# Values of an attention step as one product of 512 queries instead of two of 256

## The reference

```python
# block 1, causal
s = einsum('bhqd,bhkd->bhqk', q, k) / sqrt(8); s = where(causal, s, -inf)
o = einsum('bhqk,bhkd->bqhd', softmax(s), v)
x = x + o @ Wo; then layer norm, 512-wide gelu MLP
# block 2, not causal
attn = softmax(einsum('bhqd,bhkd->bhqk', q, k) / sqrt(8))
ao = einsum('bhqk,bhkd->bhqd', attn, v)
# then layer norm and a mixture of 8 experts, 2 chosen for each token
```

## Time and profile before

| | us |
|---|---|
| median of 3 runs | 1733.78 |
| lowest and highest run | 1729.83, 1735.24 |
| profiled execution, from first to last instruction (its own time is shown as this span alone) | 1730.5 |
| TensorE, VectorE, ScalarE busy in it | 1456.8, 1251.8, 1169.9 |
| first attention, values from/to | 116.7 to about 593 |
| second attention, values from/to | about 790 to 1468.4 |

### The profile page before, as it was taken

One profiled execution on the slowest core, in us unless ns is written; L12 is line 12 of the kernel. 1 busy time (PEld: TensorE's weight loads), 2 busy tenths in 40 slices (PEclk: granted clock), 3 DMA queues, 4 the chain that ended last, 5 costly groups with the idle time before them and its releaser, 6 DMA issues.

```text
span 1730.5 us, 39194 instructions
## 1 busy us (share of the span) xinstructions
PE 1456.8 (84%) x15185; PEld 663.6 (38%) x15185; DVE 1251.8 (72%) x1974; ACT 1169.9 (68%) x2373; POOL 339.9 (20%) x386
## 2 busy tenths in 40 slices
PE   5679999999998888748999999899988989899940
PEld 3334444444444455402222222222222223788930
DVE  6787877878776156688999999799979973342444
ACT  7537777867777655506998998789877887433421
POOL 5300000000000156400000001100112331441455
PEclk9869999989989899957999999999999999999985
DMA  4612101111110344320133332011200130767941
GB/s 137 199 57 64 68 33 60 44 57 55 54 51 19 95 125 136 118 89 8 45 116 121 125 113 81 18 47 63 75 17 32 55 125 30 208 212 240 277 139 56
DMA packets 127770, 158.46 MB, mean 92 GB/s; under 512 B 14432, under 2 KB 100448, under 8 KB 127328
## 3 DMA queue, kind: packets, MB, share of 16 engines
q1 hardware_dynamic: 118368, 130.77, 24.0%
q0 software_dynamic: 9216, 25.18, 4.1%
HBM read 90.90 MB, written 68.96 MB: 92 GB/s over the span
## 4 chain that ended last, share of the span: by engine, by line
PE 24%; DVE 17%; issue 9%; DMA 8%; ACT 4%; POOL 2%; SPq 1%; another core or an unknown queue 0%; ACTq 0%; POOLq 0%; DVEq 0%
DVE row_max L632 14%; PE bank L599 6%; DMA sorted_in<-v_all,slots 5%; PE banks L1439 4%; PE banks L1429 4%; PE banks L575 4%; PE banks L543 2%; ACT probs L686 2%; DMA qk_parts<-parts 1%; POOL probs L1250 1%; DMA parts<-sorted_in 1%; PE banks L1420 1%; PE banks L1384 0%; PE banks L330 0%; PE banks L1331 0%
## 5 line engine op out<-in xcount | busy, mean ns | idle before, releaser
L632 DVE TENSOR_REDUCE row_max<-banks 128x2 f32<-128x1024 f32 (+3 forms) x896 | 939.5, 1104 | 140.4 <-PE banks L549 74.1
L686 ACT ACTIVATE probs<-banks 128x512 f32<-128x512 f32 (+3 forms) x1792 | 879.8, 551 | 192.0 <-PE banks L575 90.1
L599 PE MATMUL bank<-probs,v_ones 128*32 128x256 f32 (+3 forms) x7168 | 539.2, 378 | 19.8 <-ACT o_sums L697 16.8
L543 PE MATMUL banks<-k_work,q_work 48*128 48x512 bf16 (+3 forms) x1792 | 368.1, 383 | 76.3 <-DVE row_max L632 57.3
L575 PE MATMUL banks<-q_work,k_work 51*128 51x512 bf16 (+3 forms) x1792 | 387.2, 375 | 43.1 <-DMA q_work<-max_T 25.4
L575 PEld LDWEIGHTS banks<-q_work,k_work 51*128 51x128 bf16 x1792 | 102.5, 93 | 414.4 <-ACT probs L686 322.6
L599 PEld LDWEIGHTS bank<-probs,v_ones 128*32 128x32 f32 x7168 | 147.5, 109 | 257.8 <-ACT probs L686 183.8
L724 POOL DMA_DIRECT2D heads_out<-o_sums x64 | 35.7, 558 | 1015.2 <-ACT o_sums L697 1015.2
L543 PEld LDWEIGHTS banks<-k_work,q_work 48*128 48x128 bf16 x1792 | 95.1, 96 | 142.7 <-DVE row_max L632 105.8
L2007 ACT ACTIVATE rope<-banks,expert 128x256 f32<-128x256 f32 x184 | 72.2, 475 | 114.8 <-PE banks L1429 89.8
L1429 PE MATMUL banks<-rope,expert 128*128 128x256 f32 x368 | 90.6, 391 | 7.8 <-issue 7.2
(11 more groups left out here) (194 smaller groups left out, 1104.9 us busy)
## 6 DMA issues: line engine op xcount, KB each, us to landing
expert<-expert_rows SPq DMA_DIRECT2D x46, 578.0 KB
qk_parts<-parts SPq DMA_DIRECT2D x64, 256.0 KB, 3.4
heads_out<-o_sums POOLq DMA_DIRECT2D x64, 256.0 KB, 4.0
sorted_in<-front SPq DMA_DIRECT2D x21, 512.0 KB, 6.3
q_work<-qk_parts SPq DMA_DIRECT2D x64, 128.0 KB
k_work<-qk_parts SPq DMA_DIRECT2D x64, 128.0 KB
parts<-sorted_in SPq DMA_DIRECT2D x46, 128.0 KB
q_work<-qk_parts SPq DMA_DIRECT2D x64, 64.0 KB
```

Source lines behind the costliest of these rows:

```text
L543: last = pe.matmul(to[:, par, 0:width], q[r:r + M0, pair, qt * P:(qt + 1) * P], k[r:r + M0, pair, kh * G:kh * G + width], start=True, stop ...
L599: last = pe.matmul(bank[7][32 * j:32 * j + 32, c0 + part * w:c0 + (part + 1) * w], v_ones[i % QB][:, kt, j, :], prob_slots[:, (e + j) % RI ...
L632: dve.tensor_reduce(row_max[:, qt, 2 * pair:2 * pair + 2, kh], self.buf_of("chunk", g, c)[:, :, 0:width], AX.X, ALU.max).then_inc(s["chunk ...
L686: act.activation(prob_slots[:, e % RING, 0:width], banks46[:, e % EXP_BANKS, 0:width], ACT.Exp, scale=SCALE).then_inc(s["exps"], 1)
```

## The change

`PARTS`, the number of products into which a step's values are cut, goes from 2 (PAIRS) to 1. Each part covers `(G - c0) // PARTS` queries, so a full step's product has 512 moving columns instead of 256. The one part is issued behind the second unit of the next step; before, one part was issued behind each unit. Semaphore counts follow PARTS everywhere else in the code.

```diff
-PARTS = PAIRS
+PARTS = 1
...
         for pair in range(PAIRS):
             order.append(("unit", 0, PAIRS * k + pair))
             some((PAIRS * k + pair + 1) * len(stream) // (PAIRS * len(steps)))
-            if k:
-                order.append(("values", 0, PAIRS * (k - 1) + pair))
+            if k and pair % (PAIRS // PARTS) == PAIRS // PARTS - 1:
+                order.append(("values", 0, PARTS * (k - 1) + pair // (PAIRS // PARTS)))
```

## The result

The changed kernel takes 1832.07 us (median of 4 runs, 1816.66 to 1854.62) against 1733.89 (4 runs, 1729.83 to 1735.24): 1.054 times as long, 95% interval 1.049 to 1.059. The ratios in this document leave out executions over 1.5% longer than the shortest of their kernel: here the one of 1854.62 us (the median of the other three is 1827.58), further down one of 1810.68 us (half of each row maximum) and one of 4056.71 us (both chunks between the units), whose length nothing in the record explains. On another chip the changed kernel took 1834.74 us, 1.060 (1.054 to 1.065). Forecast were 1819 us, 1785 to 1862. The profiled execution has a span of 1825.8 us, 95 more than before.

The account below looks back on a forecast made before the run. TensorE, VectorE and ScalarE were taken as close to full, with a hidden scores-exp-scores wait of 1.07 us that the change exposes. 61 + 24 = 85 us on 1733.8 gave 1819 us, range 1785 to 1862.

Parts of the forecast that it names:

- The loop: Second attention's steady step: odd unit's second score waits for even unit's first exp, chunk and values queue; 2.22 to 2.61 us.
- The price of 512 columns: Values product of 512 queries on TensorE: 1.00 us against 1.14 for two of 256, continued from four narrower widths.
- Rival (a): Whole kernel: TensorE's time is what counts, second score does not stop the line, faster at 1666 us; chance 5%.
- (b): Whole kernel: no change, savings and loop cancelling, 1734 us, with values near 0.65 us; chance 2%.
- (d): Values products in both attentions: long products are dear, 1.14 us in place of 1.00, total 1871 us; chance 3%.
- (e): Both attentions: loss half hidden by other VectorE and ScalarE work, or values at 0.86 us; 1767 to 1794 us; 8%.
- The idle time: TensorE idles some 0.6 us before the odd unit's second score, ScalarE some 0.5 us before a step's first exp.
- A clean group: One group at full clock: second attention 39.0 before and 43.3 us after, first attention 28.5 and 30.2 us.
- The second attention, +61 forecast: All 16 groups of the second attention: 69 us shortfall to 2.61 us steps, times 4.3 / 4.9, gives +61 us.
- the walk: A group followed through code order with measured durations and waits; second attention 39.0 us before, where the trace has 39.19.
- rival (c): Second attention: the clock falls too, one half-clock stretch in each of 16 groups, 42 us more, 1861 us; chance 10%.
- The first attention, +24 forecast: All 16 groups of the first attention: 1.7 us each, 27 us, less 3 for half-clock stretches, gives +24 us.

Follow-up runs that it names:

- half of each row maximum: Changed kernel with each row maximum taken over the first half of its chunk's keys only; 1793.52 us, 1.038 times the kernel before.
- both chunks between the units: Changed kernel with the second chunk moved ahead of the second unit in steps 2 to 6 of the second attention; 1811.7 us, 1.047.
- run with the repeated chunks: Changed kernel with the long products of the chunk behind each step's first unit issued twice; 1822.82 us, 1.056.
- the changed kernel again: Changed kernel rerun without further change, beside the others on one chip; 1834.74 us, 1.060 times the kernel before.

## Why the prediction was right, and by how much it was off

*The loop.* Forecast: second score at 1.07, chunk 1.30, values 1.61, step 2.61 us. Measured: 1.08, then values 1.61 behind the start (948.14 - 946.53), step 2.61. A step without a second chunk 2.39, as forecast. This is shown not only by the trace but by shortening the exp (2.39), by filling the gap at no cost and by moving a chunk into it (2.39).

*The price of 512 columns.* 1.00 us, from the line through four widths; measured 1.00. The 0.14 us below two products of 256 is right as a sum, but it is no saving of instructions: two products of 256 next to each other take 1.01. What is saved is what lies between products and other work, at their beginning (0.09 us) and end (0.14 us). The Trainium skill, "TensorEngine Tiling (Array Packing)", section "Key Properties", says that a change of the tiling mode drains TensorE; these rows agree with it, since the cost stands only where values meet scores or a chunk. The saving brought no time here, since TensorE's stream was no longer what counted. Rival (a) is out, and so are (b), (d) and the part of (e) with values at 0.86 us.

*The idle time.* I said some 0.6 us; the profile shows 0.25. From the first score's start at 946.98 to the second's at 947.61 it is 0.63, but the profile has the first score last 0.38 of that. The forecast measured the wait from starts, where the profile counts from the end of the instruction before. ScalarE's 0.54 us was forecast as 0.5.

*A clean group.* 43.7 us for 43.3 in the second attention: the four long steps became 3.00, 3.25, 2.81 and 4.41 as walked, and the first, from which I took 0.1, stayed at 1.76. Half of the 0.4 is the walk's start, 39.0 where the trace has 39.19. In the first attention 30.3 for 30.2.

*The second attention, +61 forecast, +81 measured.* By the clean group's 4.5 us in place of 4.3 the term becomes 69 x 4.5 / 4.9 = 63. The other 18 go with the clock: it was granted 0.93 on the mean where before had 0.97. Three ordinary groups with one stretch at half clock last 44.9 to 45.2 us; the four with front work grew by 6.4, 6.8, 2.3 and 8.6 us; the last one runs from 1538 to its end at 0.50, and there the loop's step is 3.70 us (1539.65 to 1543.35) instead of 2.39:

```profile
1539.65 0.60 PE L575 MATMUL banks<-q_work,k_work 51*128 51x512 bf16 x1 [0.26 <-ACT probs L686]
1540.19 1.93 PE L599 MATMUL bank<-probs,v_ones 128*32 128x512 f32 x8
1542.05 1.03 PE L575 MATMUL banks<-q_work,k_work 51*128 51x512 bf16 x3
1543.35 0.60 PE L575 MATMUL banks<-q_work,k_work 51*128 51x512 bf16 x1 [0.26 <-ACT probs L686]
```

That the clock is the whole of the 18 is an estimate. The run with the repeated chunks supports it: with the clock at 0.96 its second attention took 751.7 us, 71.5 more than before, and some 6 of that are its groups' extra 0.4 us, which leaves 65, near the 63.

So rival (c) came true by less than half, and not once in each group: clean groups of 43.7 us keep full clock, with TensorE busy 39.1 us or 89% and not 83 to 87%. Most of it lies in the groups with front work and in the last one.

*The first attention, +24 forecast, +14 measured.* Clean groups grew by 1.7 us as said, 27 in all. But of before's 15 groups up to the last seven lasted 31 us and more, from stretches at half clock; after, four reach 32. In other executions the changed first attention took 501 us (the changed kernel again) and 503 us (the change in this attention alone), 21 and 23 more than before, close to the 24. So the 10 us are where the clock happened to fall in the execution that was profiled, not a better kernel.

Both errors come from the clock, and they have opposite signs. Their sum, +10 us, is most of the 11 by which the span (1825.8 us for 1815) was missed. That the total came out this close is in part luck: with 501 us for the first attention and the 761 of the second it would have been 17.

*What stays open.* Which pattern of work makes the clock fall in the second attention's front groups was not tried. The values product was never fast enough to test where the decision point of rival (a) lies. A fourth bank for scores, which would let the second score go without that exp, was not tried either.

## What to carry to other kernels

An engine that works in order and feeds another through few buffers has a round trip, here 1.07 us from scores through exp to the scores that reuse the bank. Here it cost nothing as long as other work of that length stood in every gap. So spread such work evenly over the round trips, and before merging two pieces into one, add up what is left in the emptied gap. Fewer and larger instructions on the busiest engine lost 5% this way, and its share of busy time hardly showed it (84% before, 82% after): look for a pair that has come apart in the timeline, and test with work put into the gap.

## What the runs showed that I had not expected

More work on TensorE made the kernel faster. In the kernel before, 0.96 us of repeated products at each group's end of the first attention raised the granted clock there from 0.93 to 0.98 and took 17 us off 480. The stretch at half clock in the earlier trace rows had begun right after a group's end where TensorE was busy 3.41 of 5 us; with the fill such stretches went, all but at the attention's beginning and end. Groups without one last 28.6 us in both kernels, so the gain is the clock's alone. In the changed kernel the repeated chunks likewise went with a higher clock (0.98 and 0.96 for 0.96 and 0.93), and the total did not rise although its groups were 0.3 to 0.4 us longer. The clock also goes with the scatter of the changed kernel, 38 us in one series of four executions and 16 in the other, where the kernel before scatters by 5 to 13: in each series the order by time is the order by mean clock (1816.66 us at 0.920 to 1854.62 at 0.893; 1828.09 at 0.916 to 1843.91 at 0.903). What makes the clock fall in one execution and not in another no run shows.
